# A recurrent layer run as one stage in place of three, with its first convolution tap on ScalarE and its gated product on VectorE

## The reference, cut to what matters

```python
xn = _rmsnorm(x, gamma1)                               # x is the layer norm of the stream
gate, v = jnp.split(jnp.einsum('btd,hd->bth', xn, W_in), 2, axis=-1)     # 2 x 192
v = _causal_depthwise_conv(v, conv_w, conv_b)          # 4 taps along time
forget, inp = jnp.split(jnp.einsum('bth,gh->btg', v, W_gates) + b_gates, 2, axis=-1)
alpha = jnp.exp(-8.0 * jax.nn.softplus(forget_base) * jax.nn.sigmoid(forget))
beta = jnp.sqrt(1.0 - alpha ** 2 + 1e-06)
h = _linear_scan(alpha, beta * jax.nn.sigmoid(inp) * v)      # h[t] = alpha[t] h[t-1] + ...
x = x + jnp.einsum('bth,dh->btd', jax.nn.gelu(gate) * h, W_out)
xn2 = _rmsnorm(x, gamma2)
gate2, v2 = jnp.split(jnp.einsum('btd,gd->btg', xn2, W_grow), 2, axis=-1)  # 2 x 256
x = x + jnp.einsum('btg,dg->btd', jax.nn.gelu(gate2) * v2, W_shrink)
```

## Time and profile before

| what | value |
|---|---|
| median of 3 runs | 2557.7 us (2555.05 to 2560.04) |
| profiled execution, its own device time | 2552.87 us |
| profiled execution, span from first to last instruction | 2551.2 us |
| TensorE busy | 2226.8 us, 87% |
| VectorE busy | 1734.4 us, 68% |
| ScalarE busy | 1598.0 us, 63% |
| GpSimd busy | 1251.7 us, 49% |
| mean granted TensorE clock | 0.946 of full speed |

### The profile page before, as it was taken

One profiled execution on the slowest core, in us unless ns is written; L12 is line 12 of the kernel. 1 busy time (PEld: TensorE's weight loads), 2 busy tenths in 40 slices (PEclk: granted clock), 3 DMA queues, 4 the chain that ended last, 5 costly groups with the idle time before them and its releaser, 6 DMA issues. The chain is left out here.

```text
span 2551.2 us, 59915 instructions
## 1 busy us (share of the span) xinstructions
PE 2226.8 (87%) x19192; PEld 1631.1 (64%) x19192; DVE 1734.4 (68%) x4747; ACT 1598.0 (63%) x3559; POOL 1251.7 (49%) x1743
## 2 busy tenths in 40 slices
PE   5999999799789887999779888899676788887996
PEld 3666666599556665799666555589333455555795
DVE  5677777444578786544667888666777667886666
ACT  3666666377566665577548888544465268887344
POOL 3456666445234555455123566557433334665563
PEclk9999999899799999999879999899788979999998
DMA  8000000322300001222200000223300000000225
GB/s 312 30 5 12 13 12 12 100 61 71 85 2 5 16 16 47 83 70 63 70 5 2 8 18 18 73 71 83 77 1 7 1 5 2 17 18 31 87 82 136
DMA packets 133603, 116.54 MB, mean 46 GB/s; under 512 B 22903, under 2 KB 119685, under 8 KB 131264
## 3 DMA queue, kind: packets, MB, share of 16 engines
q1 hardware_dynamic: 116032, 78.17, 10.5%
q0 software_dynamic: 17280, 34.65, 4.1%
HBM read 58.22 MB, written 56.36 MB: 45 GB/s over the span
## 5 line engine op out<-in xcount | busy, mean ns | idle before, releaser
L1239 ACT ACTIVATE A_Pm<-A_t 128x768 f32<-128x768 f32 (+1 forms) x512 | 468.7, 915 | 154.5 <-PE A_t L1670 150.3
L370 POOL DMA_INDIRECT ybuf<-F_yo,F_idx x284 | 315.9, 1112 | 241.4 <-DVE F_yo L579 145.3
L1437 DVE TENSOR_REDUCE A_padm<-A_s 128x4 f32<-128x1024 f32 x264 | 322.5, 1222 | 64.9 <-PE A_s L1662 63.4
L224 POOL DMA_INDIRECT xbuf<-xs,dst x256 | 269.9, 1054 | 105.8 <-issue 60.4
L1118 POOL TENSOR_SCALAR_AFFINE_SELECT A_Pm<-A_Pm 128x512 f32<-128x512 f32 x256 | 167.6, 655 | 292.9 <-ACT A_Pm L1239 291.3
L740 PE MATMUL F_hb<-F_xT,F_wt 128*128 128x128 f32 x2272 | 306.0, 278 | 0.7 <-issue 0.2
L1697 PE MATMUL A_ot<-A_Pm,A_V 128*32 128x256 f32 (+3 forms) x3640 | 295.5, 389 | 11.0 <-POOL A_Pm L1118 10.0
L1670 PE MATMUL A_t<-A_Q,A_K 32*128 32x256 f32 (+1 forms) x2560 | 304.3, 331 | 0.0
L740 PEld LDWEIGHTS F_hb<-F_xT,F_wt 128*128 128x128 f32 x2272 | 275.6, 191 | 6.8 <-issue 2.0
L1662 PE MATMUL A_s<-A_K,A_Q 32*128 32x256 f32 (+1 forms) x1584 | 202.1, 332 | 58.5 <-DVE A_padm L1437 40.8
L752 PE MATMUL F_out<-F_WA,F_g 128*128 x1704 | 245.5, 280 | 6.1 <-DVE F_g L570 3.0
(11 more groups left out here) (428 smaller groups left out, 4983.1 us busy)
## 6 DMA issues: line engine op xcount, KB each, us to landing
F_xr<-xbuf SPq DMA_DIRECT2D x284, 68.0 KB, 1.8
xbuf<-A_zero SPq DMA_DIRECT2D x16, 1088.0 KB, 17.6
xs<-ybuf SPq DMA_DIRECT2D x32, 512.0 KB, 6.9
ybuf<-F_yo,F_idx POOLq DMA_INDIRECT x284
xbuf<-xs,dst POOLq DMA_INDIRECT x256, 2.4
F_WA<-in_L_ffn_ew SPq DMA_DIRECT2D x2, 2048.0 KB, 9.1
F_WA<-in_L_ffn_ew SPq DMA_DIRECT2D x16, 256.0 KB, 5.6
F_WA<-in_L_ffn_e_gate SPq DMA_DIRECT2D x2, 1024.0 KB, 5.6
```

The source lines that it names most:

```text
L224: pool.indirect_dma_start(out=G["XBUF"][:, :], out_offset=bass.IndirectOffsetOnAxis(ap=G["dst"][:, t, c:c + 1], axis=0), in_=G["xs"][c][:, ...
L370: pool.indirect_dma_start(out=YBUF[:, :], out_offset=bass.IndirectOffsetOnAxis(ap=idx[n][:, h:h + 1], axis=0), in_=yo[r][:, h, :], in_offs ...
L1239: act.activation(Pm[r][:, j:j + 2, :], tbank[:, :].rearrange("p (j k) -> p j k", j=2)[:, :, 0:PW], ACT.Exp, scale=SCALE).then_inc(t_free, 1)
L1437: last = dve.reduce_max(tops.rearrange("p t j -> p j t"), sbank[:, :].rearrange("p (j t k) -> p j t k", j=2, t=TPS), AX)
```

## The change

The three stages become one, still called `recurrence_stage` (tag RR, in `recurrence_layer` the only call that is left). All its work is written out block by block, in one block of the program, so that no engine meets the others at the two inner borders. The arithmetic is the same.

- Convolution of block 0 is cut: VectorE does tap 0, tap 1 and tap 2 after its steps for blocks 5, 6 and 7 of the projection part, and tap 3 after the last of them. TensorE goes from the last projection straight to `gate(0)`, whose results use the four banks of the projection; it waits there for ScalarE's last reads.
- Tap 0 of blocks 2 to 7 goes from GpSimd to ScalarE as an Identity activation with scale and bias, put behind the Sqrt of each block.
- The gated product goes from GpSimd to VectorE, put behind each scan.
- The MLP part follows in the same lists, without a hardware loop. Its first statistics and first norm stand before the last `add`, and GpSimd does its first two roots before its first two sums of X and Y.
- `gates`, `gt` and `mm` lie in the `xs` buffers, which nothing else uses here. The weights of the MLP are fetched at the start of the layer.

```diff
-def recurrence_in_stage(nc, tag, G, w):
-
+def recurrence_stage(nc, tag, G, w):
...
+            sp.dma_start(wgr[:, :], w["W_grow"]).then_inc(m_in, 16)
+            sp.dma_start(wsh[:, :, :], w["W_shrink"].rearrange("(c p) d -> p c d", p=P)).then_inc(m_in, 16)
+            sp.dma_start(g2[:, :], w["gamma2"].rearrange("(p a) -> p a", a=1)).then_inc(m_in, 16)
...
             for b in range(NBLK):
-                root(b)
+                root_in(b)
+            pool.wait_ge(rstd_ready, NBLK)
+            root_mlp(0)
+            root_mlp(1)
+            add_rows(0)
+            add_rows(1)
+            for b in range(2, NBLK):
+                root_mlp(b)
+                add_rows(b)
...
-    def first_tap(eng, b):
-        for c in range(2):
-            last = eng.tensor_scalar(taps[b % 2][:, c, :].rearrange("p (s t) -> p s t", s=2), VB[:, b, c, :, 0:SEQ], cw[:, c, 0:1], cb[:, c:c + 1], ALU.mult, ALU.add)
-        return last
-
-    with st.block() as block:
-        @block.gpsimd
-        def _(pool):
-            def tap(b):
-                pool.wait_ge(vc_ready, b - 1)
-                first_tap(pool, b).then_inc(tap_ready, 1)
-
-            def gated(b):
-                pool.wait_ge(h_ready, b + 1)
-                pool.tensor_tensor(hh[b % 2][:, :, :], hh[b % 2][:, :, :], GB[:, b, :, :], ALU.mult).then_inc(gh_ready, 1)
-
-            tap(OWN)
-            for b in range(NBLK):
-                gated(b)
-                if b + OWN + 1 < NBLK:
-                    tap(b + OWN + 1)
...
+            def first_tap(b):
+                act.wait_ge(vc_ready, b - 1)
+                for c in range(2):
+                    last = act.activation(tap_rows(b, c), VB[:, b, c, :, 0:SEQ], ACT.Identity, scale=cw[:, c, 0:1], bias=cb[:, c:c + 1])
+                last.then_inc(tap_ready, 1)
+
+            act.wait_ge(v_done, NBLK + 1)
             for b in range(NBLK):
                 decay(b)
+                if b + OWN < NBLK:
+                    first_tap(b + OWN)
...
+            def gated(b):
+                dve.wait_ge(h_ready, b + 1)
+                dve.tensor_tensor(hh[b % 2][:, :, :], hh[b % 2][:, :, :], GB[:, b, :, :], ALU.mult).then_inc(gh_ready, 1)
...
+            for b in range(NBLK - 1):
+                take_in(b + 1)
+                if b + 2 < NBLK:
+                    norm_in(b + 2)
+                if b + 4 < NBLK:
+                    stat_in(b + 4)
+                if b >= NBLK - 4:
+                    conv(0, b - NBLK + 4, b - NBLK + 4)
+            conv(0, 3)
+            conv(1)
+            scan(0)
+            for b in range(NBLK - 1):
+                gated(b)
+                if b + 2 < NBLK:
+                    conv(b + 2)
+                add(b)
+                scan(b + 1)
+            gated(NBLK - 1)
+
+            dve.wait_ge(m_in, 48)
+            stat_mlp(0)
+            stat_mlp(1)
+            norm_mlp(0)
+            add(NBLK - 1)
+            take_mlp(0)
+            norm_mlp(1)
+            stat_mlp(2)
+            take_mlp(1)
...
-        recurrence_in_stage(nc, "RI", H, w)
         recurrence_stage(nc, "RR", H, w)
-    gated_mlp_stage(nc, "RM", G, w)
```

More of the change, by code:

```diff
@@ L2083, in recurrence_in_stage @@
     xn, xT = sb("xn", [P, TPB, D]), sb("xT", [P, 2, BLK])
[L2084 to L2088, removed]
+    taps, vc, al, hh = [[sb(f"{n}{k}", [HC, 2, BLK]) for k in range(2)] for n in ("taps", "vc", "al", "hh")]
@@ L2143, in _ @@
                 last.then_inc(v_done, 1)
[L2145 to L2214, removed]
-            def step(b, p, ahead=True):
-                pe.wait_ge(xT_ready, b + 1)
-                pe.wait_ge(gate_done, b + 1)
-                project(b, p, 0, gate_psum)
-                if ahead:
-                    turn(b + 1)
-                pe.wait_ge(v_done, b + 1)
-                project(b, p, 2, v_psum)
-            turn(0)
-            for b in range(NBLK):
-                step(b, b % 2, b + 1 < NBLK)
@@ L2316, in conv @@
                 part = lambda a, c: a[q][:, c, :].rearrange("p (s t) -> p s t", s=2)
-                for k in range(1, CONV):
+                for k in range(max(first, 1), last_tap + 1):
                     dst = vc if k == CONV - 1 else taps
@@ new lines, in turn, with project_in @@
+            def turn(b, ready, full):
+                pe.wait_ge(ready, b + 1)
+                for t in range(TPB):
+                    last = pe.transpose(xb[:, t * P:(t + 1) * P], xn[:, t, :], ident[:, :])
+                last.then_inc(full, 1)
+            def project_in(b, first, full):
+                for k in (first, first + 1):
+                    last = pe.matmul(ub[k][0:HC, :], win[:, k * HC:(k + 1) * HC], xT[:, b % 2, :], start=True, stop=True)
+                last.then_inc(full, 1)
@@ L2541, in _ @@
+            pe.wait_ge(m_in, 48)
+            turn(0, m_xn_ready, m_xT_psum)
+            gates_mlp(0)
+            values_mlp(0)
+            turn(1, m_xn_ready, m_xT_psum)
+            for b in range(NBLK - 1):
+                gates_mlp(b + 1)
+                shrink(b)
+                values_mlp(b + 1)
+                if b + 2 < NBLK:
+                    turn(b + 2, m_xn_ready, m_xT_psum)
             shrink(NBLK - 1)
```

356 lines of the change are left out of this document (178 added, 178 removed).

## The result

The changed kernel takes 2530.09 us, the median of 4 runs (2527.14 to 2543.55), against 2558.87 us for the kernel before (4 runs, 2555.05 to 2565.77). The ratio is 0.9904, with a 95% interval of 0.9884 to 0.9925: it is faster by 1.0%, some 25 us (19 to 30 by the interval). The forecast was 2532.5.

The account below looks back on a forecast made before the run. VectorE was taken to bound the recurrence blocks (busy 12.31 of 12.45 us) but not the two borders. Gains of 9.9, 7.8 and 7.2 us sum to 24.9, taking 2557.7 to 2532.8, stated as 2532.5; 8-in-10 range 2525 to 2544.

Parts of the forecast that it names:

- First border: From the end of the last projection to the start of the first scan: 9.9 us gained.
- No relief for VectorE (rival): In the blocks, taps stay slow for another reason than GpSimd: block 13.8 us, 16.2 us lost, 2549; chance 7%.
- the blocking: In the blocks, VectorE's taps stand still while GpSimd's product runs; without it the three taps cost 2.70 us less.
- ScalarE as the bound (rival): In the blocks, ScalarE becomes the bound: blocks stay at 12.44 us, 8.0 us of gain lost, 2540.8; chance 12%.
- The blocks' term: From the first scan's start to the last's: 84.2 us becomes 76.4, 7.8 us less.
- TensorE: 16 records of 0.43 and a projection of some 2.0, at full clock: TensorE's work per block of the recurrence: 9.0 of 11.1 us, so it is not late.
- The rival with TensorE at the low clock: In the blocks, TensorE stays at 1.2 GHz and is the bound at 17.8 us per block: 2573; chance 5%.
- Second border: From the last scan's start to the first `take`: 16.1 us becomes 8.9, 7.2 us less.
- What I left at nothing: The cut convolution's cost in the projection part and the MLP from `take` to the end: no change counted.

Follow-up runs that it names:

- e10: Changed kernel with block 0's convolution not cut into the projection part but whole behind its last copy; one run, 2531.3 us.
- e1: Changed kernel with tap 0 and the gated product both back on GpSimd, so the merged stage alone; 2540.5 us, 0.9932 of the kernel before.
- e3: Changed kernel with only the gated product back on GpSimd; 2538.2 us, 0.9928 of the kernel before.
- e8: Changed kernel plus a GpSimd product of two on-chip operands behind each scan, into a buffer nobody reads; one run, 2538.5 us.
- e9: Changed kernel plus two GpSimd memsets behind each scan, only writing, into a buffer nobody reads; one run, 2535.3 us.
- second profile: The changed kernel measured and profiled once more, without any edit; 2533.4 us, 0.9893 of the kernel before.
- e6: Changed kernel with filler matmuls in TensorE's gaps in the recurrence part; 2526.1 us, 0.9876 of the kernel before.
- e2: Kernel before, its three stages kept, with tap 0 moved to ScalarE and the gated product to VectorE; 2550.3 us, 0.9979 of the kernel before.
- e4: Changed kernel with only tap 0 back on GpSimd; 2532.9 us, 0.9904 of the kernel before.
- e7: Changed kernel with two more Identity activations behind each tap 0 on ScalarE, into a buffer nobody reads; one run, 2535.5 us.

## Why the prediction was right, step by step

**First border: right.** 12.9 us where I had 13.3. TensorE, ScalarE and VectorE came in the order worked out; e10 and e1 show that this gain is the merged stage's and doesn't hang on the moves.

**No relief for VectorE (rival), against the blocking: settled.** The block fell from 12.44 to 10.99 (11.1 forecast), all taps take 0.74 us, and e3, e8 and e9 show that it is GpSimd's reading that had held them. GpSimd's product beside VectorE cost it 2.1 us per block; done on VectorE it costs 1.14 to 1.26. The Trainium skill ("Perfetto Trace Analysis", "Optimizing Scalar/DVE Operations") says that moving some work off a saturated VectorE, to ScalarE or even GpSimd, may make sense, but that between VectorE and GpSimd it might not help, since they share a read port. The traces agree with the second part: with the product on GpSimd (e3) the block is 11.81 us, with it on VectorE 10.99.

**ScalarE as the bound (rival): did not happen.** ScalarE needs 10.0 us per block; my sum of 10.5 was 0.5 too high, for overlap of neighbours. Tap 0 on ScalarE took 1.50 for the pair, in the range of 1.1 to 1.6.

**The blocks' term: mis-sized.** 7.8 us forecast, 4.1 measured, 4.4 in the second profile. The step that failed is "TensorE: 16 records of 0.43 and a projection of some 2.0, at full clock" for the blocks behind the third. The argument for it was that TensorE had longer gaps before and kept a clock of 1.00 with them. That misread the row: it has TensorE busy for 11.13 of 12.45 us, idle for 1.3 and not 3.4. The next two blocks of the kernel before, idle for 3.3 and 1.9 us, already show a clock of 0.86, and in each a gate of 8.80 us in place of 7.11:

```profile
1907.40:1919.80 12.40, 9.13 (x29) 4.22 (x28) 12.26 (x15) 7.10 (x9) 5.63 (x3) 0.86 0.00 0
1919.80:1932.20 12.40, 10.54 (x33) 4.92 (x32) 12.26 (x14) 8.79 (x10) 5.65 (x3) 0.86 0.00 0
```

```profile
1914.38 8.80 PE L2365 MATMUL RR_g<-RR_vc,R_wg 96*96 96x512 f32 x16 [2.03 <-DVE RR_vc L2320]
...
1926.83 8.80 PE L2365 MATMUL RR_g<-RR_vc,R_wg 96*96 96x512 f32 x16 [1.86 <-DVE RR_vc L2320]
```

There VectorE, the bound, hid it. After the change the clock fell at the end of a gap of 2.17 us, and the last step, which has no taps to hide `gate(7)`, took 12.89 in place of 9.2, all of the 3.7 us missing. Of these, 3.3 are the clock's (`gate(7)` 10.43 in place of 7.11; with it at 7.11 in e6 the step is 9.57). The other 0.4 are missing at the high clock too: `gate(7)` ends 4.1 us behind scan 6 in e6 where I had 3.8, and behind it the scan waits for ScalarE's chain to the Sqrt, which I had left out of this step. Two other slowed gates cost 1.0 (block 1 to 2, of which I had 0.6) and 0.3; the steps where no gate is slow are each 0.1 shorter than the 11.1 forecast, which cancels these. The rival with TensorE at the low clock had the right mechanism with the wrong extent: slow in a part of three blocks, not in all. e6 shows it directly: with the gaps filled the blocks take 75.5.

**Second border: right.** 8.78 us against 8.9. In e1 and e3, with the product on GpSimd, it is 9.6, so the product's move gives 0.8 of the 7.3 (in the three stages of e2 it gives 1.2 of 16.1).

**What I left at nothing.** The MLP and the projection part gained 0.4 and 1.1 us in the first profile. Over all profiles of kernels in this study without fillers, the projection part lies between 40.8 and 42.3 and the MLP between 57.9 and 59.2, so these two are no effects that one profile can tell. That they made up for 1.5 of the 3.7 us missing from the blocks is luck.

**Open.** Why the clock falls before `gate(7)` in three profiles of the same order of blocks is not settled. The length of the gap before it does not decide it alone: 2.17 us in the three, 2.10 and 2.16 in e4 and e7, where `gate(7)` took 7.11, and 2.17 before `gate(4)` of the changed kernel, which took 7.11 too. In e8 and e9 it was `gate(6)` that took longer (9.59 and 8.80 us), in e3 it was `gate(7)` behind a gap of only 1.39 (8.80), and in e10 `gate(7)` took 10.28.
